# Two groups of the shared network move beside attention's last tiles

## The reference

```python
x = layernorm(x + attention(x))                     # 8 x 1024 tokens, 512 wide: x1
scores = softmax(x1 @ gate_w.T)                     # 64 experts, top 6
# an expert takes at most 128 tokens, in order of token; the rest is dropped
h  = silu(xe @ w1[e].T) * (xe @ w3[e].T)            # 352 wide
routed = sum over the 6 experts of gate * (h @ w2[e].T)
z  = (silu(x1 @ sw1.T) * (x1 @ sw3.T)) @ sw2.T      # shared network, 704 wide, every token
out = layernorm(routed + z)
```

## Time and profile before

| what | value |
|---|---|
| three runs, median (lowest to highest) | 3597.3 us (3596.38 to 3597.97) |
| the profiled execution's own time | 3600.05 us |
| its span, first to last instruction | 3598.3 us |
| mean granted TensorE clock | 0.966 of full |
| busy: PE, DVE, ACT, POOL | 3248.1, 2501.9, 1969.8, 1379.8 us |
| attention's tail: 2143 to 2297 of the span | PE busy 64.8 of 154 us |
| expert stage: from 2297 | first expert matmul at 2345.74 |
| pure groups: from about 3322 | 276 us to the end |

### The profile page before, as it was taken

The page is one execution under the profiler, slowest core; times in us unless marked ns, Lnnn a source line. Parts: engine busy times, 40 slices in busy tenths (PEclk is TensorE's granted clock), DMA queues, the critical chain, the costliest instruction groups (busy, mean ns, idle before and its releaser), DMA issues. The chain is left out here.

```text
span 3598.3 us, 57246 instructions
## 1 busy us (share of the span) xinstructions
PE 3248.1 (90%) x17410; PEld 2594.5 (72%) x17410; DVE 2501.9 (70%) x3686; ACT 1969.8 (55%) x3440; POOL 1379.8 (38%) x2129
## 2 busy tenths in 40 slices
PE   8999995899999999999999995199999999999996
PEld 7888883677777777777777764078888888888775
DVE  6777775899999999999998982155555555554433
ACT  2222224787777877877777771154555555553332
POOL 0000001046666666666676767322222222232111
PEclk9999997999999999999999996599999999999998
DMA  6666665456656656666565552357777777776654
GB/s 249 224 227 222 228 221 157 121 151 163 163 156 162 164 154 167 159 157 170 147 164 159 157 141 74 109 179 212 212 211 208 214 211 215 212 211 201 217 175 123
DMA packets 338382, 644.68 MB, mean 179 GB/s; under 512 B 39056, under 2 KB 137936, under 8 KB 333536
## 3 DMA queue, kind: packets, MB, share of 16 engines
q1 hardware_dynamic: 300000, 574.51, 52.2%
q0 software_dynamic: 35840, 50.60, 8.1%
q10 hardware_dynamic: 2304, 16.78, 1.1%
HBM read 422.90 MB, written 219.09 MB: 178 GB/s over the span
## 5 line engine op out<-in xcount | busy, mean ns | idle before, releaser
L652 ACT ACTIVATE att_prob<-att_ps_s,att_neg_max 128x1024 f32<-128x1024 f32 x512 | 570.6, 1116 | 146.4 <-DVE att_neg_max L762 130.8
L762 DVE TENSOR_REDUCE att_neg_max<-att_ps_s 128x1 f32<-128x1024 f32 x512 | 600.6, 1215 | 44.5 <-PE att_ps_s L539 43.3
L539 PE MATMUL att_ps_s<-att_k,att_q 64*128 64x512 f32 x3072 | 433.2, 413 | 73.2 <-ACT att_prob L652 38.6
L850 POOL DMA_INDIRECT slots<-att_entry,att_slot x384 | 419.7, 1093 | 154.8 <-issue 98.7
L539 PEld LDWEIGHTS att_ps_s<-att_k,att_q 64*128 64x128 f32 x3072 | 288.3, 187 | 178.0 <-issue 143.5
L706 DVE SCALAR_TENSOR_TENSOR att_diff<-att_prob,att_weight 128x1024 f32<-128x1024 f32 x256 | 346.8, 1355 | 9.1
L1388 POOL DMA_INDIRECT total<-exp_ye,exp_rows x64 | 108.1, 1689 | 585.5 <-ACT exp_ye L1235 467.6
L499 PE MATMUL att_ps_t<-att_ident,att_diff 128*128 128x128 f32 x2048 | 288.4, 278 | 18.7 <-ACT att_diff_lo L598 18.7
L76 PE MATMUL exp_ps_ab<-exp_x_t,exp_sw_hi 128*128 128x512 f32 x616 | 248.5, 403 | 36.4 <-DVE exp_sw_lo L1506 24.9
L620 ACT CAST att_diff_hi<-att_ps_t 128x1024 fp32r<-128x1024 f32 x256 | 259.1, 1012 | 32.2 <-PE att_ps_t L499 32.2
L499 PEld LDWEIGHTS att_ps_t<-att_ident,att_diff 128*128 128x128 f32 x2048 | 232.7, 141 | 53.0 <-ACT att_diff_lo L598 37.6
(11 more groups left out here) (264 smaller groups left out, 8405.9 us busy)
## 6 DMA issues: line engine op xcount, KB each, us to landing
exp_loaded<-in_w_t SPq DMA_DIRECT2D x64, 1408.0 KB, 6.2
att_k<-k_parts SPq DMA_DIRECT2D x260, 256.0 KB, 5.3
att_v<-v_parts SPq DMA_DIRECT2D x64, 1024.0 KB
att_q<-q_parts SPq DMA_DIRECT2D x260, 128.0 KB, 4.9
v_parts<-proj_v_out SPq DMA_DIRECT2D x64, 512.0 KB, 3.3
x_parts<-att_x_t SPq DMA_DIRECT2D x64, 512.0 KB, 2.9
exp_loaded<-in_w_t SPq DMA_DIRECT2D x64, 512.0 KB, 4.4
exp_x_t<-x_parts SPq DMA_DIRECT2D x14, 2048.0 KB, 12.7
```

The lines of the kernel that those rows point to most:

```text
L539: last = nc.tensor.matmul(ps_s[s][:, cols], q_buf[q % 2][rows, q_part, q_cols], k_buf[q % 2][rows, k_part, cols], start=m == 0, stop=m == 2)
L652: nc.scalar.activation(prob[s][i][:], ps_s[s][:], ACT.Exp, bias=neg_max[:, s, i : i + 1], accum_out=total).then_inc(exp_done[s], 1)
L762: nc.vector.tensor_reduce(neg_max[:, s, i : i + 1], ps_s[s][:], AX.X, ALU.max, negate=True).then_inc(max_done[s], 1)
L850: nc.gpsimd.indirect_dma_start(slots, bass.IndirectOffsetOnAxis(ap=slot[four][:, c : c + 1], axis=0), entry[four][:, c, :], None, bounds_c ...
```

## The change

The shared network becomes a class `SharedNet` whose buffers and semaphores live through `attend` and `experts`. Its weights take the room of attention's q, k, v and `diff` buffers once these are read; the raw weights take that of `prob` and `diff`; its PSUM is that of the scores. In attention's tail ("last") the raw weights are loaded at the end of SP's turns 2, 4, 5 and 7 and split at the end of ScalarE's and DVE's turns 3, 5, 6 and 8. Groups 0 and 1 are cut into 20 whole pieces (`PIECES`): `PIECE_AT` puts them at the end of TensorE's turns 9, 10, 13, 14, ... 29, 30 (12 pieces: all of group 0 and two units of group 1) and the eight others behind the last turn. ScalarE and DVE do their part of a piece one turn later. POOL adds both groups' z behind its last scatters. SP loads the first expert's weights at the end of `attend`. The mixed groups are then 2 to 12 (with the same experts and plans), the pure ones 13 to 15, with five final norms each. `up`, `down`, `act_unit`, `dve_hid`, `dve_hid_low`, `z_copy` and `add_z` move into the class as they were.

```diff
+FRONT = 2
+class SharedNet:
+    def load_weights(self, sp, step):
+        if step < 2:
+            sp.dma_start(self.w13_raw, self.sw13_t[:, step * SHARED : (step + 1) * SHARED].rearrange("(k p) n -> p k n", p=P)).then_inc(self.shared_w13_in, DMA)
+        elif step == 2:
+            sp.dma_start(self.w2_raw, self.sw2_t[0 : 3 * P, :].rearrange("(k p) n -> p k n", p=P)).then_inc(self.shared_w2_in, DMA)
...
+    def weights_high(self, act, step):
+        if step < 2:
+            act.wait_ge(self.shared_w13_in, DMA * (step + 1))
+        else:
+            act.wait_ge(self.shared_w2_in, DMA * (1, 4)[step - 2])
+        self.nc.scalar.copy(self.weights_of(0, step), self.w13_raw if step < 2 else self.w2_raw).then_inc(self.split_hi, 1)
+    def weights_low(self, dve, step):
+        dve.wait_ge(self.split_hi, step + 1)
+        raw = self.w13_raw if step < 2 else self.w2_raw
+        self.nc.vector.tensor_tensor(self.weights_of(1, step), raw, self.weights_of(0, step).bitcast(F32), ALU.subtract).then_inc(self.split_lo, 1)
...
 def attend(...):
+        LOADS = {2: 0, 4: 1, 5: 2, 7: 3}
+        SPLITS = {3: 0, 5: 1, 6: 2, 8: 3}
+        LAST_TURNS = SLOT - QT + 1
+        PIECES = [(g, piece) for g in range(FRONT) for piece in ["0", "1", "2", "3", "4", "5", "z0", "z1", "z2", "z3"]]
+        FIRST_PIECE = 9
+        OPEN = [jl for jl in range(FIRST_PIECE, LAST_TURNS + len(PIECES)) if jl % QT in (1, 2) or jl >= LAST_TURNS]
+        PIECE_AT = dict(zip(OPEN, PIECES))
+        X_LOADS = {jl + 1: g + 1 for jl, (g, piece) in PIECE_AT.items() if piece == "5"}
+        END = max(PIECE_AT) + 1
+        def sp_front(sp, jl):
+            if jl == 2:
+                sp.wait_ge(t_done, BATCH * STEPS)
+                sp.wait_ge(value_done, BATCH * QUADS - 1)
+                sp.wait_ge(parts_stored, DMA * (TILES_ALL - GATE // QT + 1))
+                sh.load_x(sp, 0, 0, sh.x_t)
+            if jl in LOADS:
+                step = LOADS[jl]
+                if step in (1, 3):
+                    sp.wait_ge(sh.split_lo, step)
+                sh.load_weights(sp, step)
+            if jl in X_LOADS:
+                sp.wait_ge(sh.up_done, UNITS * (X_LOADS[jl] + 1))
+                sh.load_x(sp, X_LOADS[jl], 0, sh.x_t)
+        def pe_front(pe, jl):
+            if jl in PIECE_AT:
+                sh.pe_piece(pe, *PIECE_AT[jl])
+        def act_front(act, jl):
+            if jl in SPLITS:
+                act.wait_ge(s_done[1], BATCH * STEPS)
+                act.wait_ge(value_done, BATCH * QUADS - (1 if SPLITS[jl] < 2 else 0))
+                sh.weights_high(act, SPLITS[jl])
+            if jl - 1 in PIECE_AT:
+                sh.act_piece(act, *PIECE_AT[jl - 1])
+        def dve_front(dve, jl):
+            if jl in SPLITS:
+                sh.weights_low(dve, SPLITS[jl])
+            if jl - 1 in PIECE_AT:
+                sh.dve_piece(dve, *PIECE_AT[jl - 1])
+        def pool_front(pool, g):
+            for t in range(TT):
+                sh.add_z(pool, g, t)
+            pool.wait_ge(sh.z_added, DMA * TT * (g + 1))
+            pool.sem_inc(sh.z_free, TT)
         def pe_turns(pe, b, mode):
...
+                if mode == "last":
+                    pe_front(pe, jl)
...
                 sp_turns(sp, BATCH, "last")
+                for jl in range(LAST_TURNS, END + 1):
+                    sp_front(sp, jl)
+                sp.wait_ge(sh.split_lo, 4)
+                load_experts(sp)
...
                 pool_hit_pos(pool, TILES_ALL - 1)
+                for i in range(2):
+                    pool.wait_ge(x1_stored[i], 2 * DMA * (TILES_ALL // 2))
                 pool_scatter(pool, TILES_ALL - 1, TILES_ALL - 1)
+                for g in range(FRONT):
+                    pool_front(pool, g)
 def experts(...):
-    PURE = list(range(MIXED + 1, GROUPS))
+    PURE = list(range(FRONT + MIXED + 1, GROUPS))
-        FINISH = {g: list(range(3 * q, 3 * q + 3)) for q, g in enumerate(PURE)}
+        FINISH = {g: list(range(5 * q, 5 * q + 5)) for q, g in enumerate(PURE)}
         def act_pure(act, g):
...
-                    act_finish(act, FINISH[g - 1][2])
-                if u in (2, 4):
-                    act_finish(act, FINISH[g][u // 2 - 1])
+                    act_finish(act, FINISH[g - 1][4])
+                if u >= 2:
+                    act_finish(act, FINISH[g][u - 2])
         def dve_pure(dve, g):
...
-                if u % 2:
-                    dve_finish(dve, FINISH[g][u // 2])
+                if u:
+                    dve_finish(dve, FINISH[g][u - 1])
...
-                with sp.Fori(0, MIXED) as g:
+                with sp.Fori(FRONT, FRONT + MIXED) as g:
```

More of the change, by code:

```diff
@@ L49 @@
 DMA = 16
+FULL = SHARED // P
+REST = SHARED - FULL * P
+UNITS = FULL + 1
+GROUPS = TOKENS // CHUNK
+TT = CHUNK // P
+HT = -(-INTER // P)
+FRONT = 2
+assert REST == HALF
 class Stage:
@@ L370, in attend @@
         ps_s = [st.psum(f"ps_s{s}", [P, SEQ]) for s in range(2)]
+        sh.ps_ab = [bank[:].rearrange("p (a c) -> p a c", a=2) for bank in ps_s]
+        sh.z_buf = [wo_raw[:, t, :] for t in range(TT)]
         ps_t = st.psum("ps_t", [P, TILES, P])
@@ L900, in _ @@
                 act_turns(act, BATCH, "last")
+                for jl in range(LAST_TURNS, END + 1):
+                    act_front(act, jl)
             @block.vector
@@ L925, in _ @@
                 dve_turns(dve, BATCH, "last")
+                for jl in range(LAST_TURNS, END + 1):
+                    dve_front(dve, jl)
             @block.gpsimd
@@ new lines, in load_first, with load_second, experts @@
+def load_first(sp, sh, w13_t, e):
+    sp.dma_start(sh.w13_raw, w13_t[e].rearrange("(k p) n -> p k n", p=P)).then_inc(sh.w13_in, DMA)
+def load_second(sp, sh, w2_t, e):
+    last = INTER - (HT - 1) * P
+    sp.dma_start(sh.w2_raw[:, 0 : HT - 1, :], w2_t[e, 0 : (HT - 1) * P, :].rearrange("(k p) n -> p k n", p=P)).then_inc(sh.w2_in, DMA)
+    sp.dma_start(sh.w2_raw[0:last, HT - 1, :], w2_t[e, (HT - 1) * P : INTER, :]).then_inc(sh.w2_in, DMA)
+def experts(nc, sh, x1, slots, w13_t, w2_t, ident_in, total, out):
@@ L966, in experts @@
     SIX, FOUR, MIXED = 6, 4, 10
[L967 to L969 removed]
+    PURE = list(range(FRONT + MIXED + 1, GROUPS))
     LAST = INTER - (HT - 1) * P
     FIN = 3
[L972 removed]
+    assert SIX * MIXED + FOUR == EXPERTS
     with Stage(nc, "exp") as st:
[L974 to L975 removed]
@@ L1477, in _ @@
                 act.sem_inc(ye_done, 1)
-                for i in range(2):
-                    act.wait_ge(shared_in, (2 + 4 * i) * DMA)
-                    nc.scalar.copy(sw13[0][:, :, i * SHARED : (i + 1) * SHARED], w13_raw).then_inc(split_hi, 1)
-                    nc.scalar.copy(sw2[0][:, 3 * i : 3 * i + 3, :], w2_raw).then_inc(split_hi, 1)
                 w13_high(act, 0)
-                with act.Fori(0, MIXED) as g:
+                with act.Fori(FRONT, FRONT + MIXED) as g:
                     act_group(act, g, PLAN6, False)
-                act_group(act, MIXED, PLAN4, True)
+                act_group(act, FRONT + MIXED, PLAN4, True)
                 for g in PURE:
                     act_pure(act, g)
-                act_finish(act, FINISH[PURE[-1]][2])
+                act_finish(act, FINISH[PURE[-1]][4])
                 act_finish(act, GROUPS - 1)
@@ L1550, in layer, with load_experts @@
     project(nc, x_t, w_qk, w_v, (rope[0], rope[2]), (rope[1], rope[3]), q_parts, k_parts, v_parts)
-    attend(nc, q_parts, k_parts, v_parts, x, lambdas, subln, w_out, gate_t, ident, before, empty_slots, x1, x1_parts, total, slots)
-    experts(nc, x1, x1_parts, slots, w13_t, w2_t, sw13_t, sw2_t, ident, total, out)
+    def load_experts(sp):
+        load_first(sp, sh, w13_t, 0)
+        load_second(sp, sh, w2_t, 0)
+    with Stage(nc, "sh") as st:
+        sh = SharedNet(nc, st, x1_parts, total, sw13_t, sw2_t)
+        attend(nc, sh, q_parts, k_parts, v_parts, x, lambdas, subln, w_out, gate_t, ident, before, empty_slots, x1, x1_parts, total, slots, load_experts)
+        experts(nc, sh, x1, slots, w13_t, w2_t, ident, total, out)
 def shape_constants():
```

347 lines of the change are left out of this document (173 added, 174 removed).

## The result

| | median, us | lowest to highest |
|---|---|---|
| before, 4 runs | 3597.64 | 3596.38 to 3599.51 |
| changed, 4 runs | 3553.95 | 3547.18 to 3562.63 |

The ratio is 0.9879, with a 95% interval of 0.9857 to 0.9902: faster by 44 us (1.2%) where 57 were predicted. The time lies 14 us above the predicted 3540, within the range of 3510 to 3580. The profiled execution of the changed kernel is the slowest of its four (3562.63 us, span 3560.9). So the first question is what in its span belongs to the change and what to that execution.

What follows compares the result with a forecast made beforehand. TensorE was taken to bound the pure groups at the end and to be half free or idle in attention's tail. Terms -85 + 19 + 11 + 28 - 31 = -58 us gave about 3540 us, range 3510 to 3580.

Steps and rivals of the forecast that it cites:

- Parts 1 and 2: End of kernel: two pure groups removed, -95.4 us; the three that stay carry five final norms each, +10; together -85.
- over 8: Pure groups: POOL's z additions averaging over 8 us was named as a sign that the prediction was wrong.
- Rival (c): Pure groups: POOL's additions become the bound, 3572 us; chance 0.08 without loss, 0.04 with loss.
- Part 3: Attention's tail: splitting raw weights in ScalarE's and DVE's queues delays the position sum and POOL's slots, +19 us.
- Rival (d): Attention's tail: the weight splits stay serial with the tile's ring, part 3 at +42 us, 3563 in all; chance 0.08.
- Part 4: Attention's tail: shared-network pieces between tiles lengthen three tiles to 66.5 us in all, +11 us.
- z0 to z3 ... cost nothing: Attention's tail: these z tiles fall into waits for ScalarE and POOL and cost nothing; without that cover 15.6 us.
- Part 5: Behind attention's last tile: the second group takes 58 us to the next stage where 30.2 passed, +28 us.
- rival (b): Attention's tail and second group: TensorE's clock stays low, 70 us more, 3610, or 3568 with the tail alone; chance 0.08.
- Part 6: Expert stage's start: without the shared weights the first expert matmul comes 18 us in instead of 48.5, -31 us.
- The table loads: Attention's tail: ScalarE's switches between exponential and Silu counted at 0; by the skill's page an estimated 4 us more.
- (a): Attention's tail takes the work for less: loads land early, part 3 +9, part 4 -5, 3514 us; chance 0.14.

Runs made afterwards that it cites:

- e7: Changed kernel with one shared-network group instead of two beside attention's last tiles, the second returned to the pure groups at the end: 3557.9 us, ratio 0.9873.
- e3: Changed kernel with no piece between attention's tiles, all 20 pieces run behind the last turn: 3582.8 us, ratio 0.9953.
- e1: Changed kernel with the four weight splits spread over four tiles and moved under the output product: 3533.3 us, ratio 0.9826.
- e6: Changed kernel with POOL awaiting the landing of the second group's additions in the experts' stage, not at attention's end: 3550.7 us, ratio 0.9867.
- e15: Changed kernel with splits under the product, second group's z tiles and first group's landing wait past the boundary, first expert's weights behind the table load: 3514.3 us.
- e12: Changed kernel with splits under the product, second group's z tiles and the wait for the first group's landing past the boundary: 3525.0 us, ratio 0.9780.
- e10: Changed kernel with splits under the product, second group's z tiles past the boundary, one piece per tile moved from turn 2 to turn 3: 3520.0 us.
- e9: Changed kernel with splits under the product, second group's z tiles past the boundary, one piece per tile moved from turn 2 to turn 0: 3523.7 us.

## Why the prediction was right, and where it was not

**Parts 1 and 2** (-85, measured -86.8) hold, in sum and by their steps: with five norms the two full distances are 51.7 and 52.9 us where 47.7 + 3.5 was the guess, and the additions met other transfers more often, as said. The chain of waits shows it for the second pure group:

```profile
3471.45 8.02 DMA total<-exp_z
...
3480.14 3.88 DMA total<-exp_z
...
3484.68 9.06 DMA total<-exp_z
...
3494.41 4.08 DMA total<-exp_z
```

Two of four are slow, 25.0 us in sum, where the group in the earlier trace rows has one slow one and 20.8 in sum. Over the twelve additions of the three groups the mean is 5.6 us from issue to landing ("over 8" would have been wrong). Rival (c) falls. What I did not see is how the saving divides: e7 gives 276.4 - 226.1 = 50.3 us for the first group and 36.5 for the second.

**Part 3** (+19) holds. From tile 58's product to that of tile 60, two tiles that hold the splits, 54.3 us passed where 37.1 did: +17.3. e3, which has the splits but no pieces between the tiles, gives 136.6 - 119.1 = 17.5, and e1 takes back 15.8. The mechanism is the one named, DVE's queue in order: DVE stood idle for 7.3 us (9 predicted), and the position sum came 9.3 us late (10 predicted) against tile 58's product. The two tiles divide otherwise than I had it (6.9 and 10.4 where the parts put 10 and 9). Rival (d), 42 us, falls.

**Part 4** (+11) holds in the three tiles that it counted: from the product of tile 60 to that of tile 63 67.7 us passed where 56.7 did, +11.0. One by one they took 22.9, 23.8 and 21.0 us where 25, 21 and 20.5 were put, so that here as in part 3 errors of opposite sign met in the sum, and its closeness is partly luck. And "z0 to z3 ... cost nothing" was wrong by 4.3 us: from the last product to the last position matmul 29.7 us passed, 25.4 before. These rows show where, the first of PE before, the others of POOL and PE in the changed kernel:

```profile
2250.60 1.09 PE L564 MATMUL att_ps_m<-att_ident,att_x 128*128 128x128 f32 x4 [4.38 <-ACT att_x L635]
...
2287.57 1.03 POOL L1037 TENSOR_TENSOR att_hit_pos<-att_hit,att_routed 128x384 f32<-128x384 f32 x1
2288.54 0.21 POOL L1011 TENSOR_TENSOR att_var_eps<-att_mean_var,att_eps_col 128x1 f32<-128x1 f32 x1
...
2292.60 0.60 PE L786 MATMUL att_ps_m<-att_ident,att_x 128*128 128x128 f32 x4
```

x1 is turned 13.1 us behind the last product, 8.9 before (that product is at 2279.51, and was at 2241.71). ScalarE's activation ahead of it starts 2.7 us later behind the product, because POOL, still at the slots of an earlier tile, comes to the LayerNorm only at 2288.54 without having waited; and TensorE, in z0 and z1 until 2292.6, takes x1 up 1.5 us later behind that activation. In sum the tail is 2.6 us longer than predicted.

**Part 5** (+28, measured +37.5) is the step that failed, in two terms of its sum. "The stage boundary, about 2", with 5.5 for the last copy, addition and landing, was mis-sized: these 7.5 us took 15.0. e6 shows 3.6 of them to be the landing. The copy and the addition's issue end 2.6 us behind the start of the last matmul, and the remaining 8.8 lie between POOL's last DMA issue and the next stage, with nothing running. The rows had it: the kernel before needed 8.2 us from its last scatter to the next stage, and I named this number without using it. The other term is the matmuls and their wait, 52.7 us where 50.4 were counted: behind each of the two waits TensorE restarts at 0.43 us a matmul, for 7 and 14 matmuls of 0.2 us more. That is also what is left of rival (b): the clock window values are 0.73 to 0.91, not near 1, because the products and the restarts run at the low level, while the units between run at 0.23. In the last group it costs 4.5 us, not the 42 of 200 matmuls.

**Part 6** (-31, measured -30.3) holds: the first expert matmul came 18.5 us behind the stage's start, 18 predicted. The five experiments that start this stage in the same way have the stretch at 988.1 to 992.9, 1.5 to 6.3 us below the changed kernel's, so the measured figure is good to some 6 us.

**The table loads.** ScalarE changes between exponential and Silu; in ACT's timeline of the changed kernel:

```profile
2244.82 0.81 ACT L857 ACTIVATE att_x<-att_summed,att_shift,att_rstd 128x512 f32<-128x512 f32 x1 [11.04 <-POOL att_shift L1016]
2245.65 1.28 ACT L201 ACT_TABLE_LOAD   x1
2246.95 0.60 ACT L201 ACTIVATE sh_plain_room<-att_ps_s 128x512 f32<-128x512 f32 x1
```

The load stands between two activations with 0.02 us on either side, so this switch costs 1.28 us. The Trainium skill ("ScalarE: Activation LUTs", What ACT_TABLE_LOAD costs) adds 1.38 us for a drain; this row shows none, and the row decides. In sum the tiles came out near the predicted length with the loads counted at 0; no run here leaves the loads out.

**The rivals.** (a) fell: the loads did not land early, and no part came out at its lower bound. It names the right place, though: e1, with the same splits behind the product and spread over four tiles, keeps some 2 us of part 3 where (a) hoped for 9.

## What to carry to other kernels

Work that goes into an engine's queue costs what stands behind it there: the same four splits cost 17 us in front of a position sum and some 2 us spread over later waits of 5 us that the same engine has under each product, so look in the old trace for the waits on every engine that the new work passes, not only on the one with most room. What is moved to the end of a stage also pays that stage's boundary, which is read from the old trace between its last instruction and the next stage's first; and a wait on the other side of the boundary is a better place. Cut the trace at marks that both kernels have before explaining a difference: here one row of five, 9.5 us, was clock dips of that execution and no part of the change.

## What the runs showed of the hardware

The end of a stage is dear where POOL issues the last DMA. From the end of that issue to the next stage pass 8.2 us before, 8.8 in e6, 9.4 in e15 and 9.9 in e12, where the landing is not awaited in POOL's queue, and 12.2 to 16.1 in the ten executions where it is. (In e12 and e15 DVE's last work also comes late, 5.4 and 5.0 us ahead of the stage, so before and e6 show POOL's part alone.) Behind the other engines the stage can follow sooner, as these rows of e10's POOL, DVE and SP timelines show:

```profile
2309.83 3.73 POOL L237 DMA_DIRECT2D total<-att_wo_raw  x4
...
2322.75 0.69 DVE L232 TENSOR_TENSOR sh_room<-sh_plain_room,sh_room 64x512 fp32r<-64x512 f32 x1 [0.68 <-ACT sh_room L205]
...
2327.57 0.34 SPq L1581 DMA_DIRECT2D exp_ident<-in_ident  x1
```

DVE ends 4.1 us ahead of the stage, POOL's issue 14.0 (5.0 and 14.0 in e9). What POOL does in the 8 to 10 us that are no landing, no run here shows.

TensorE's granted clock also falls in steady attention: to 0.87 over 40 us in which the engine was busy for 37.7. These falls stand behind short idle times for which the profile names no other engine ("issue"). In the changed kernel the clock is at its lower level, 1.2 GHz, for 10.2 us from 957.2 and from 1356.5, and its PE timeline has:

```profile
956.58 2.43 PE L761 MATMUL att_ps_s<-sh_room 64*128 64x512 f32 x12 [1.87 <-issue]
...
1355.59 2.16 PE L761 MATMUL att_ps_s<-sh_room 64*128 64x512 f32 x12 [1.78 <-issue]
```

Between 710 and 2130 us each of the 14 executions has six such idle times, some 198 us apart and 1.6 to 2.0 us long. Eleven of the 84 are followed by a fall (those are 1.8 to 2.0 us long), and no fall stands elsewhere there; which ones it hits differs from execution to execution, and why, no run shows. The changed kernel's falls between 640 and 720 stand behind waits of 1.5 to 1.6 us for ScalarE's exponentials. The mark at tile 58 lies 12.7 us apart between the earliest and the latest execution.
